# A decoder layer on one core: batch 0's cross-attention queries and keys made during the last pairs of the self-attention

## The reference, cut to what matters

```python
x = layernorm(x + self_attention(x))        # 4 heads of 64, learned window mask
x = layernorm(x + cross_attention(x, ctx))  # 16 heads of 16, 361 keys
x = layernorm(x + experts(x))               # top 2 of 8, silu(g) * u
# self-attention: q_in = x @ Wq.T; q, k, v = q_in @ Wqkv.T + bqkv
#   dx = sigmoid(relu(q_in) @ Wop.T @ W2.T + b2) * L
#   scores masked where the distance exceeds dx + window, softmax, times v
# cross-attention: Q = x @ wq.T + bq, K = ctx @ wk.T + bk, V = ctx @ wv.T + bv
#   softmax(Q K.T / 4) V, then @ wo.T + bo
```

## Time and profile before

| | |
|---|---|
| median of the timed runs | 663.26 us |
| profiled execution | 663.6 us |
| its span | 661.5 us |
| TensorE busy | 622.6 us (94%) |
| VectorE busy | 373.1 us (56%) |
| ScalarE busy | 315.1 us (48%) |
| GpSimd busy | 292.3 us (44%) |
| TensorE's granted clock over the span | 0.979 of full speed |

### The profile page before, as it was taken

One profiled execution on the slowest core, in us unless ns is written; L12 is line 12 of the kernel. 1 busy time (PEld: TensorE's weight loads), 2 busy tenths in 40 slices (PEclk: granted clock), 3 DMA queues, 4 the chain that ended last, 5 costly groups with the idle time before them and its releaser, 6 DMA issues.

```text
span 661.5 us, 16872 instructions
## 1 busy us (share of the span) xinstructions
PE 622.6 (94%) x5901; PEld 531.3 (80%) x5902; DVE 373.1 (56%) x996; ACT 315.1 (48%) x813; POOL 292.3 (44%) x526
## 2 busy tenths in 40 slices
PE   6999977999999998999999989999999999999994
PEld 5999954677777776777667768899999999999994
DVE  1778786777777876778767867322222222222245
ACT  2455452777777766777667676121121222112124
POOL 5245365334363349443773342424343342425244
PEclk9999996999999998999989999999999999999998
DMA  8232204565666644444443348688676777666443
GB/s 269 84 93 75 64 28 129 155 193 179 204 191 192 196 135 106 125 119 114 120 107 93 99 140 297 221 274 224 202 211 226 231 231 220 211 195 204 179 138 139
DMA packets 72897, 109.36 MB, mean 165 GB/s; under 512 B 9786, under 2 KB 50562, under 8 KB 72066
## 3 DMA queue, kind: packets, MB, share of 16 engines
q1 hardware_dynamic: 66882, 100.40, 48.7%
q0 software_dynamic: 5952, 8.14, 5.4%
HBM read 73.77 MB, written 12.44 MB: 130 GB/s over the span
## 4 chain that ended last, share of the span: by engine, by line
PE 50%; DMA 19%; issue 10%; DVE 7%; POOLq 6%; POOL 6%; ACT 2%; SPq 0%; DVEq 0%; ACTq 0%
DMA accd<-y,si 18%; PE ps L1603 7%; PE ps L1655 6%; PE ps L1677 6%; PE ps L1630 5%; POOLq L725 5%; PE ps L1614 5%; PE ps L1535 3%; PE ps L1698 2%; PE ps L1663 2%; PE ps L1524 2%; PE ps L1543 2%; PE ps L804 1%; PE ps L1580 1%; POOL r_ln L365 1%
## 5 line engine op out<-in xcount | busy, mean ns | idle before, releaser
L2160 DVE TENSOR_REDUCE cmx<-ps 100x1 f32<-100x361 f32 x256 | 134.6, 531 | 62.9 <-PE ps L1603 58.7
L804 PE MATMUL ps<-xsT,W 128*128 128x128 f32 x1408 | 164.5, 276 | 0.0
L804 PEld LDWEIGHTS ps<-xsT,W 128*128 128x128 f32 x1408 | 160.6, 192 | 0.3
L1930 ACT ACTIVATE cpr<-ps 128x300 f32<-128x300 f32 x256 | 104.8, 419 | 58.2 <-PE ps L1614 57.7
L1603 PE MATMUL ps<-st 96*100 96x361 bf16 x256 | 86.5, 341 | 5.7 <-DVE cmx L2160 4.5
L1614 PEld LDWEIGHTS ps<-st 120*128 120x128 bf16 x768 | 63.2, 102 | 31.9 <-issue 9.3
L853 PE MATMUL ps<-WD,hT 128*128 x384 | 88.1, 380 | 0.5 <-issue 0.5
L1614 PE MATMUL ps<-st 120*128 120x100 bf16 x768 | 77.2, 209 | 3.6 <-ACT st L1935 1.6
L853 PEld LDWEIGHTS ps<-WD,hT 128*128 128x128 f32 x384 | 70.7, 191 | 8.8 <-issue 0.5
L1008 DVE TENSOR_SCALAR y<-ps,wt 128x256 f32<-128x256 f32 x28 | 13.5, 484 | 106.3 <-PE ps L853 106.3
L719 POOL DMA_INDIRECT accd<-y,si x28 | 44.9, 1605 | 64.2 <-DMA accd<-y,si 55.9
(11 more groups left out here) (267 smaller groups left out, 1026.8 us busy)
## 6 DMA issues: line engine op xcount, KB each, us to landing
W<-in_wgu SPq DMA_DIRECT2D x32, 1408.0 KB, 6.5
st<-parts SPq DMA_DIRECT2D x192, 115.2 KB, 2.5
WD<-in_wd SPq DMA_DIRECT2D x6, 1024.0 KB, 5.6
cx<-in_ctxT SPq DMA_DIRECT2D x16, 361.0 KB, 4.5
x_sb<-in_x SPq DMA_DIRECT2D x8, 200.0 KB
x1d<-x SPq DMA_DIRECT2D x8, 200.0 KB
x1Td<-x1T SPq DMA_DIRECT2D x8, 200.0 KB, 3.3
x1T_sb<-x1Td SPq DMA_DIRECT2D x16, 100.0 KB, 3.5
```

Of the source, the lines that this page charges most:

```text
L804: mm = pe.matmul(out[:, i * P:(i + 1) * P], self.columns(t, k, c), self.xsT[:, t.par, k, :], start=(k == 0), stop=(k == KC - 1))
L1930: act.activation(pr[:, h % (2 * HG), :], ps[:, B_T + h % 2, 0:NCH * L], ACT.Exp).then_inc(exp_ok, 1)
L2160: dve.tensor_reduce(mx[:, half, hh:hh + 1], ps[0:L, B_S + h % 2, 0:CTX], AX_X, ALU.max).then_inc(max_ok, 1)
```

## The change

Batch 0's queries are made in pair 4 and its keys in pairs 5 and 6, into bank 0, the bank of the self-attention's q_in, ahead of `turn_probs`; TensorE waits for `dx_ev` of the same pair first, and `q_in` of the next pair waits for ScalarE's copy. The load of x1T moves from pair 4 to pair 3. The first cast moves from VectorE to ScalarE (`cast`) for batches 0 and 1; the other parts of batch 0 are made in pairs 5 to 7, its stacks sent in pairs 6 and 7. `softmax_in(7)` stands ahead of `a_normalise(6)` on VectorE; `a_normalise(7)` moves into lap -1, at head 5. Batch 1's keys and queries follow `scores(7)`, its rests and third parts stand at heads 0, 1, 3 and 4 of lap -1. x1 of pairs 6 and 7 is transposed at heads 6 and 12 of lap -1.

```diff
+        def keys_bank(b, m):
+            return M0 + m if b else B_QIN
 @sync
-                    if g == 4:
+                    if g == 3:
                         sp.wait_ge(x1T_out[0], 16)
                         load_x1T(0)
                         load_x1T(1)
-                    if g == PAIRS - 1:
-                        stack(0, 0)
-                        stack(0, 1)
+                    if g >= PAIRS - 2:
+                        stack(0, g - PAIRS + 2)
...
-                store_T(PAIRS - 2)
...
                         a_store(PAIRS - 1)
+                        store_T(PAIRS - 2)
                         store_T(PAIRS - 1)
 @gpsimd
                     add_bias(g)
+                    if g >= PAIRS - 2:
+                        copy_first(0, g - PAIRS + 2)
                     if g < PAIRS - 1:
                         finish(g - 1)
-                copy_first(0, 0)
                 finish(PAIRS - 2)
-                copy_first(0, 1)
                 pool.wait_ge(cross_in, 16 * cross.LOADS)
                 pool.tensor_copy(bvr[:, :, :], ...)
+                copy_first(1, 0)
+                copy_first(1, 1)
                 finish(PAIRS - 1)
 @tensor, q_in
                     wait(pe, dx_ev, g)
+                    if g == PAIRS - 3:
+                        pe.wait_ge(q_ev, 1)
+                    if g > PAIRS - 3:
+                        pe.wait_ge(k_ev, g - PAIRS + 3)
 @tensor, pairs
-                    if g == PAIRS:
-                        pe.wait_ge(k_ev, 1)
-                        keys(1, 0)
+                    if PAIRS - 4 <= g < PAIRS - 1:
+                        pe.wait_ge(dx_ev, g + 1)
+                    if g == PAIRS - 4:
+                        pe.wait_ge(cross_in, 16 * cross.LOADS)
+                        queries(0)
+                    if g == PAIRS - 3:
+                        keys(0, 0)
+                    if g == PAIRS - 2:
+                        keys(0, 1)
                     if 1 <= g <= PAIRS:
                         turn_probs(g - 1, 0)
-                    if g == PAIRS - 1:
-                        pe.wait_ge(cross_in, 16 * cross.LOADS)
-                        pe.wait_ge(dx_ev, PAIRS)
-                        keys(0, 0)
-                    if g == PAIRS:
-                        pe.wait_ge(q_ev, 1)
-                        queries(1)
-                    if 1 <= g <= PAIRS:
                         turn_probs(g - 1, 1)
-                    if g == PAIRS:
-                        pe.wait_ge(k_ev, 2)
-                        keys(1, 1)
...
                     if g == PAIRS - 1:
+                        pe.wait_ge(dx_ev, PAIRS)
+                        keys(1, 0)
+                    if 2 <= g < PAIRS:
+                        turn_x1(g - 2)
+                    if g == PAIRS - 1:
                         pe.wait_ge(qk_ev, 2 * PAIRS)
-                        queries(0)
-                        keys(0, 1)
-                    if 2 <= g <= PAIRS:
-                        turn_x1(g - 2)
+                        queries(1)
+                        keys(1, 1)
 @tensor, laps
-                        if h == 8 and i < 0:
+                        if h == 6 and i < 0:
+                            turn_x1(PAIRS - 2)
+                        if h == 12 and i < 0:
                             turn_x1(PAIRS - 1)
 @scalar
+                def cast(b, m):
+                    act.wait_ge(k_ev, 2 * b + m + 1)
+                    act.wait_ge(q_ev, b + 1)
+                    wait(act, kq_in[m], 16 * SLOTS * b)
+                    act.activation(parts[:, m, 4, :], kf[:, m, :], ACT.Copy).then_inc(k1_ok, 1)
 @scalar, pairs
                         v_out(g)
+                    if g == PAIRS - 4:
+                        act.wait_ge(cross_in, 16 * cross.LOADS)
+                        act.mul(bq4[:, :], bqk_sb[:, 0:KC], 1.0 / np.sqrt(DH)).then_inc(act_set, 1)
+                        act.wait_ge(act_set, 2)
+                        queries_out(0)
+                    if PAIRS - 3 <= g < PAIRS - 1:
+                        keys_out(0, g - PAIRS + 3)
...
                         relu(g + 1)
+                    if PAIRS - 2 <= g:
+                        second_part(0, g - PAIRS + 2)
+                    if PAIRS - 3 <= g < PAIRS - 1:
+                        cast(0, g - PAIRS + 3)
                     if 2 <= g < PAIRS - 1:
                         x1T_copy(g - 2)
+                keys_out(1, 0)
                 x1T_copy(PAIRS - 3)
                 a_exps(PAIRS - 1, 0)
+                queries_out(1)
                 a_exps(PAIRS - 1, 1)
                 probs_out(PAIRS - 1, 0)
+                keys_out(1, 1)
                 probs_out(PAIRS - 1, 1)
+                cast(1, 0)
+                cast(1, 1)
+                second_part(1, 0)
+                second_part(1, 1)
 @vector, pairs
                     masks(g)
+                    if g == PAIRS - 1:
+                        third_part(0, 1)
+                        softmax_in(g)
                     if g >= 1:
                         a_normalise(g - 1)
+                    if g == PAIRS - 2:
+                        third_part(0, 0)
+                    if PAIRS - 3 <= g < PAIRS - 1:
+                        rest(0, g - PAIRS + 3)
 @vector, laps
+                        if h < 2 and i < 0:
+                            rest(1, h)
+                        if 3 <= h < 5 and i < 0:
+                            third_part(1, h - 3)
+                        if h == 5 and i < 0:
+                            a_normalise(PAIRS - 1)
```

57 lines of the change are left out of this document (18 added, 39 removed).

## The result

| | before | after |
|---|---|---|
| median of the timed runs | 663.24 us (661.37 to 663.93) | 676.25 us (675.85 to 677.29) |
| profiled execution | 663.6 us | 677.29 us |
| its span | 661.5 us | 675.2 us |
| TensorE's granted clock over the span | 0.979 | 0.972 |
| VectorE busy | 373.1 us | 372.7 us |

The changed kernel takes 1.0202 times as long (95% interval 1.017 to 1.0234), 13.0 us more by the medians. The forecast was 2.2 us more, with 668.4 as the upper end of its range. So the direction was right and the size was not. Of the twelve timed executions of E10 further down, two (667.89 and 3460.85 us) were slow ones and are left out of its figures.

What follows compares the result with a forecast made beforehand. It took TensorE as the bound, with 9.2 us idle and some 6 us lost to low clock before the first transposed scores. Terms 86.25 + 18.7 + 18.3 = 123.25 against 121.06, 2.2 us later: 665.5 us, range 661.6 to 668.4.

Steps and rivals of the forecast that it cites:

- GpSimd's first copies are later than before: Lap -1: batch 0's second half still lands some 2 us before head 8 wants it, so the lateness costs nothing.
- the split just behind the norm of pair 7: Lap -1, GpSimd: norm of 4.25 us ends 13.5 us after the first maximum, the queued split at 14.5.
- rival 1: Pair 7: the clock falls there too; about 4 us of low clock cost some 1.5 us, giving 667.0; chance 0.18.
- with the rest I take 1.65 us, bounds 1.2 and 1.9: Pair 7, VectorE: time for third_part(0, 0) and rest(0, 1) ahead of pair 6's softmax.
- The rule that the prediction weighed: TensorE's clock: only a stretch idle throughout lowers it, so lap -1 would stay high; the prediction said the trace contradicts this.
- The second rival: Lap -1: the clock stays high, GpSimd's split limits, the lap takes 16.95 us and the kernel 664.1; chance 0.16.
- Work for 3.45 us: Pairs 4 to 6, TensorE: queries(0), keys(0, 0) and keys(0, 1) moved earlier, the same work as before.
- The waits: Pairs 4 to 6, TensorE: 2.35 us waiting for dx_ev with semaphores, and 0.6 us for the load of x1T.
- the first maximum comes nearer to A: From the start of pair 7's projections (A) to batch 0's first row maximum: 18.7 us instead of 28.0.
- the start of pair 7 "near 86.3": Sign at the end of pairs 4 to 6: pair 7's projections start near 86.3 us, against 79.85 before.
- the first maximum "near 105": Sign at point M, batch 0's first row maximum on VectorE: near 105 us instead of 107.9.
- K "near 123": Sign at the end of lap -1: batch 0's first transposed scores (K) come near 123 us, against 121.06 before.

Runs made afterwards that it cites:

- E10: E8 plus 31 small unused matmuls (fillers) at heads 0 to 9 of lap -1: 661.18 us, 0.9963 of the kernel before.
- E1: Changed kernel with GpSimd's copy_first(0, 1) ahead of add_bias(7) instead of behind it: 672.80 us, 1.0135 of the kernel before.
- E5: Changed kernel with batch 1's rest(1, 1) and third_part(1, 1) behind pair 7's norm, and ScalarE's cast(1, 1) behind second_part(1, 0): 671.94 us.
- E11: Changed kernel with a_normalise(6) again ahead of pair 7's third part and softmax on VectorE: 671.97 us, 1.0137 of the kernel before.
- E8: Changed kernel with E1, E2, E3 and E5's order, plus batch 0's rests and third parts moved into VectorE's idle time ahead of the norms: 665.30 us.
- E2: Changed kernel with ScalarE's window_out ahead of the second exponential in pairs 4 to 6 too: 674.32 us, 1.0156 of the kernel before.
- E3: Changed kernel with batch 0's and 1's loads of x1T ahead of pair 3's load of x and store_T(1): 674.91 us, 1.0174.

## Why the prediction was wrong

The direction rested on the right reading, that the change pays in pair 7 and gives back in lap -1. The size was off by 10.75 us of the sum: 1.8, 4.0 and 4.95 in its three stretches.

**The lap, 4.95 us: the step that failed** is "GpSimd's first copies are later than before, since add_bias(7) waits for pair 6's norm, but batch 0's second half lands some 2 us before head 8 wants it: nothing, and as much as it is late beyond that". The lateness was seen and its cause was right. But only one of those who wait for that stack was looked at, the query scores of head 8. The other is the next writer of the same tile: `cast(b, m)` has `wait(act, kq_in[m], 16 * SLOTS * b)` in the diff itself, and `rest(1, 1)` at head 1 stands behind it. The stack landed 5.84 us behind M (117.15 - 111.31), while ScalarE was free for the cast at 109.9, before M. E1, E5 and E11 took the chain away in three ways, and the laps were 17.93, 17.54 and 16.87 us. The rest of the lap was right in its order: GpSimd's timeline after has the split just behind the norm of pair 7, as forecast,

```profile
124.95 0.23 POOL L1402 TENSOR_SCALAR a_ve<-a_mv 100x2 f32<-100x2 f32 x1 [4.72 <-DVE a_mv L2138]
...
126.09 2.44 POOL L1409 TENSOR_SCALAR x<-a_xr,a_mv,a_rstd 100x256 f32<-100x256 f32 x2
128.47 0.20 POOL L1420 CAST mxp<-cmx 100x8 bf16<-100x8 f32 x1
```

the value projections take 1.71 us in the chain (row 127.11), the constant's product 1.11 us (1.2 forecast). Two details were off, and no run here prices them. GpSimd's norm took 3.5 us, not 4.25, and the split was done at 129.5, before TensorE, at the low clock with two value projections in hand, came to `turn_maximum` at 131.58. And the clock fell at 111.7, already 0.4 us behind M, not 3 us.

**Pair 7, 4.0 us: rival 1 came true.** The prediction gave it a chance of 0.18 and a price of 1.5 us. TensorE was idle 1.16, 1.35 and 0.72 us, where the prediction had 0.4, 1.3 and 0.95; the clock fell with the weighing at 98.25. The rival's term "about 4 us of low clock cost some 1.5 us" was mis-sized: the clock was low for 6.8 us, and the weighing, scores and `keys(1, 0)` took 2.93, 1.66 and 2.52 us. Between the start of the weighing and that of the softmax it was 4.61 us instead of 2.44, so 2.2 us on the path at this point alone. Another 1.1 us are an earlier step: "with the rest I take 1.65 us, bounds 1.2 and 1.9" for third part and rest. They took 2.6 us (90.08 to 92.68), outside the bounds, while `add_bias(6)` and `copy_first(0, 0)` ran beside them on GpSimd (from 89.63): the third part rose to 1.98 us against 0.69 in E8. The softmax's second subtraction took 0.78 instead of 0.57, beside GpSimd's norm of pair 5. I had bounded the third part by one row in which it took 1.29 us. The last 0.8 us are behind the softmax: TensorE came to `turn_probs(7)` late, and ScalarE had `keys_out(1, 1)` between its two copies of the probabilities. That E8 measured 18.19 us for this stretch does not bear its sum out: E8 has less ahead of the weighing than the prediction put there and more behind it.

The rule that the prediction weighed here, of the Trainium skill, "TensorE: Matmul & The Clock Gate", section "HAM oscillation — how this bites in real kernels", asks that TensorE have no long idle gap; that only such a gap makes the clock fall is how the prediction read it. The rows speak against this reading: in the changed kernel it fell in pair 7 with no idle piece over 1.35 us, and in the lap with query scores still coming. The second rival, a lap at the high clock, did not happen by itself in any kernel.

**Pairs 4 to 6, 1.8 us.** Work for 3.45 us was right. The waits came to 3.63 us (1.38, 0.41, 1.84) against 2.95: 0.2 less in pair 5, 0.7 more in pair 6, where `rest(0, 0)` beside `add_bias(5)` took 1.32 us, not 0.64 (row 76.49), and 0.2 more in pair 4, where the DMA came last. And each of the three insertions costs some 0.37 us that no wait shows: values to `turn_probs` lose 0.17 of their overlap, `q_in`, which now wants ScalarE's copy, starts 0.91 to 0.98 us behind `turn_probs` instead of 0.82, and the keys take 1.32 us from start to start, not 1.24. The prediction had these at nothing.

**What was right.** TensorE's idleness in pairs 4 to 6 and its source (E2), the load of x1T as the next wait (E3), that the first maximum comes nearer to A (5.3 us, of 9.3 forecast), the low clock in the lap, the split behind GpSimd's norm, the laps behind K unchanged. Of the prediction's own tests, the start of pair 7 "near 86.3" failed (88.59), the first maximum "near 105" (111.31, and not by pairs 4 to 6 alone) and K "near 123" (134.56).

## What to carry to other kernels

When a step is delayed, list every reader and every next writer of its output, not only the reader that wants it for the result: the tile here had one copy, so its next writer waited first, and all behind it on VectorE and TensorE waited too. A move to an engine that idles is only free if the shared work on other engines does not slow it, and its length is to be taken from a row with the same neighbour. And before work is moved to fill idle time on TensorE, try what a few idle matmuls give: here they gave the old order as much as the best version of the move had.
